# Map loads merged and moved to ScalarE's queue in the final pass of a spectral convolution with hyperbolic normalization

## What is computed

```python
def reference(x, w_re, w_im, bias, gamma, beta):
    x = x + _L0_conv_ref(_gn(x), w_re, w_im, bias)   # group norm, rfft2, 32 x 17 modes mixed per head, irfft2, + bias
    x = x + _L1_conv_ref(_gn(x), gamma, beta)        # group norm, hyperbolic normalization over channels
    return x
```

## Time and profile before

| | us |
|---|---|
| median of 3 runs | 3985.61 (3980.61 to 3986.04) |
| profiled execution, its own time | 4024.94 |
| its span in the trace | 4023.4 |
| busy in the span: PE, DVE, ACT, POOL | 3002.5, 2748.0, 2141.8, 1513.6 |
| TensorE's granted clock, mean | 0.878 of full speed |

### The profile page before, as it was taken

How to read it: one execution, slowest core, us unless ns; L and a number is a source line. 1 busy time by engine, 2 the same in 40 slices (tenths; PEclk the granted TensorE clock), 3 DMA queues, 4 the chain that set the end, 5 groups by cost and what they waited for, 6 DMA issues and landing times. The chain is left out here.

```text
span 4023.4 us, 77883 instructions
## 1 busy us (share of the span) xinstructions
PE 3002.5 (75%) x26018; PEld 1495.1 (37%) x26018; DVE 2748.0 (68%) x2969; ACT 2141.8 (53%) x2940; POOL 1513.6 (38%) x876
## 2 busy tenths in 40 slices
PE   6988898989446767677715877877777778877776
PEld 3555555555211222222203434344333344443332
DVE  1888888888865355555444767677777677777766
ACT  6777676767200011111014767677776677776665
POOL 0110101010111111111113766666666666666666
PEclk9988888988668888888857999999999999999999
DMA  9878777677269999999915989899999899999898
GB/s 373 287 256 282 260 265 274 244 285 253 76 259 354 325 341 376 362 361 374 334 53 183 337 313 329 313 325 321 313 315 320 306 330 334 329 334 311 311 314 288
DMA packets 280512, 1199.08 MB, mean 298 GB/s; under 512 B 35145, under 2 KB 37038, under 8 KB 197934
## 3 DMA queue, kind: packets, MB, share of 16 engines
q1 hardware_dynamic: 266126, 1152.07, 79.9%
q0 software_dynamic: 14112, 43.37, 3.4%
HBM read 883.53 MB, written 311.73 MB: 297 GB/s over the span
## 5 line engine op out<-in xcount | busy, mean ns | idle before, releaser
L1323 POOL TENSOR_TENSOR c_ot<-c_ot,c_pp 128x1024 f32<-128x1024 f32 x512 | 1211.8, 2368 | 727.0 <-DVE c_ot L1272 651.8
L1262 DVE SCALAR_TENSOR_TENSOR c_xt<-c_xt,keep_k,c_p_u 128x1024 f32<-128x1024 f32 x512 | 654.0, 1277 | 332.5 <-DMA c_xt<-in_x 170.8
L1118 PE MATMUL c_p_u<-c_mv,c_zc 64*128 64x256 f32 x4096 | 612.3, 420 | 225.1 <-DVE c_xt L1262 163.1
L1272 DVE SCALAR_TENSOR_TENSOR c_ot<-c_p_f,keep_k,c_xt 128x1024 f32<-128x1024 f32 x512 | 657.3, 1284 | 177.0 <-DMA out<-c_ot 134.4
L1198 ACT ACTIVATE c_pp<-c_p_p,c_cols 128x1024 f32<-128x1024 f32 x512 | 570.5, 1114 | 362.4 <-PE c_p_p L1132 359.0
L1205 ACT ACTIVATE c_sq<-c_xt,c_cols 128x1024 f32<-128x1024 f32 x512 | 584.2, 1141 | 139.5 <-DVE c_xt L1262 138.8
L1118 PEld LDWEIGHTS c_p_u<-c_mv,c_zc 64*128 64x128 f32 x4096 | 371.4, 195 | 532.9 <-DVE c_xt L1262 321.3
L327 ACT ACTIVATE a_junk<-a_xt 128x1024 bf16<-128x1024 f32 x512 | 537.2, 1053 | 28.8 <-DMA a_xt<-in_x 21.5
L246 PE MATMUL a_p_rows<-a_xt,a_dft_h 128*64 128x512 f32 x2048 | 517.5, 652 | 33.6 <-DMA a_bias_t<-in_bias 19.5
L1132 PE MATMUL c_p_f<-c_rt,c_lwc 64*128 64x512 bf16 x1024 | 328.0, 402 | 179.6 <-DVE c_ot L1272 161.3
L663 PE MATMUL b_p_al<-b_xt,b_awc 128*32 128x512 f32 x2048 | 312.4, 682 | 161.2 <-DMA b_xt<-in_x 116.3
(11 more groups left out here) (209 smaller groups left out, 3029.8 us busy)
## 6 DMA issues: line engine op xcount, KB each, us to landing
a_xt<-in_x SPq DMA_DIRECT2D x256, 1024.0 KB, 8.0
b_xt<-in_x SPq DMA_DIRECT2D x128, 2048.0 KB, 16.0
c_xt<-in_x SPq DMA_DIRECT2D x256, 1024.0 KB, 16.7
out<-c_ot SPq DMA_DIRECT2D x256, 1024.0 KB, 18.4
maps<-b_maps POOLq DMA_DIRECT2D x64, 192.0 KB, 5.7
dmap<-b_dmap POOLq DMA_DIRECT2D x16, 768.0 KB, 11.6
c_rt<-maps SPq DMA_DIRECT2D x512, 24.0 KB
c_dmap<-dmap SPq DMA_DIRECT2D x16, 768.0 KB, 17.2
```

The costliest lines, as they stand in the source:

```text
L1118: last = nc.tensor.matmul(p_u[:, 512 * at + W * r:512 * at + W * r + W], zc[t // CH][64 * at:64 * at + 64, i], mv[t % NB][64 * at:64 * at ...
L1262: V.scalar_tensor_tensor(out=u, in0=u, scalar=kc, in1=p_u[:], op0=ALU.mult, op1=ALU.add).then_inc(u_done, 1)
L1272: V.scalar_tensor_tensor(out=ot[t % NB][:, at], in0=p_f[:], scalar=kinv, in1=xt[t % NB][:, at], op0=ALU.add, op1=ALU.mult).then_inc(f_done, 1)
L1323: P.tensor_tensor(o, o, pp[n][:], ALU.add).then_inc(o_done, 1)
```

## The change

The order of the rows in `rt` is changed: a list `MAP_ROWS` gives for each of the three parts a first row and a step, so that the rows of both halves of the partitions lie on one line: 12 rows from 58 in steps of 1, 8 rows from 15 in steps of 14, 4 rows from 36 in steps of 20. The placing of the weights in `misc` follows. The six map loads of a tile become three, each of which fills both halves; the two `bmap` loads stay. All five are issued by ACT, behind `shift(b, t, 1)` and ahead of `square(b, t, 1)`, for tile t + 4 (before: by SP, for tile t + 2), with no wait of their own: `shift(b, t, 1)` has already waited on the `f_mm` that frees the buffer. At the start of the stage ACT waits on `c_in` and issues the loads of four tiles, ahead of its first `copy_part`. SP keeps `x`, the output and the rest, and no longer waits on `c_in` there. The four stores of channel 0 of an image become one.

```diff
+MAP_ROWS = ((58, 1), (15, 14), (36, 20))
...
-    maps_v = io["maps"].rearrange("b m s (t n) -> b t (m s) n", n=TC)
+    maps_v = io["maps"].rearrange("b (a m) s (t n) -> b t a (m s) n", a=2, n=TC)
...
-            def load_maps(b, t):
-                if not (is_at(b, 0) and t < NB):
-                    sp.wait_ge(f_mm, b * GR + 2 * (t - NB) + 2)
...
-                for at in range(2):
-                    for row, rows in ((0, 6), (6, 4), (10, 2)):
-                        sp.dma_start(r[64 * at + row:64 * at + row + rows], maps_v[b, t, 6 * at:6 * at + rows]).then_inc(r_in[t % NB], 16)
-                    sp.dma_start(m[64 * at + M2:64 * at + M2 + 2].rearrange("p (n r) -> p n r", n=2), bmap_v[b, t, at]).then_inc(r_in[t % NB], 16)
...
-                for j in range(4):
-                    sp.dma_start(o0_v[b, 0, j], o0[32 * j:32 * j + 32]).then_inc(o0_out, 16)
+                sp.dma_start(o0_v[b, 0], o0[:]).then_inc(o0_out, 16)
...
-                        load_maps(b, t + 2)
...
-            sp.wait_ge(c_in, 16 * (2 + 2 * NB))
-            for t in range(2):
-                load_maps(0, t)
...
-                    pe.wait_ge(r_in[t % NB], b * (128 * T // NB) + 128 * (t // NB) + 128)
+                    pe.wait_ge(r_in[t % NB], b * (80 * T // NB) + 80 * (t // NB) + 80)
...
+            def load_maps(b, t):
+                if t >= T:
+                    b, t = b + 1, t - T
+                r, m = rt[t % NB], mv[t % NB]
+                for (first, step), rows in zip(MAP_ROWS, (6, 4, 2)):
+                    act.dma_start(r[first:first + step * (2 * rows - 1) + 1:step], maps_v[b, t, :, :rows]).then_inc(r_in[t % NB], 16)
+                for at in range(2):
+                    act.dma_start(m[64 * at + M2:64 * at + M2 + 2].rearrange("p (n r) -> p n r", n=2), bmap_v[b, t, at]).then_inc(r_in[t % NB], 16)
...
                     shift(b, t, 1)
+                    if not (last and t + NB >= T):
+                        load_maps(b, t + NB)
...
             act.wait_ge(zeroed, 2 * NB + 2)
+            act.wait_ge(c_in, 16 * (2 + 2 * NB))
+            for t in range(NB):
+                load_maps(0, t)
             act.wait_ge(filled, 3)
```

More of the change, by code:

```diff
@@ L83, in constants @@
     m[:, 10] = np.where(p // 2 == 0, 1.0, -1.0)
[L84 to L87, removed]
+    for a, at in enumerate((12, 18)):
+        for part, ((first, step), rows) in enumerate(zip(MAP_ROWS, (6, 4, 2))):
+            for i in range(rows):
+                m[first + step * (rows * a + i), at + 2 * part + i % 2] = 1.0
     c["misc"] = m
@@ L1022, in load_x @@
                 sp.dma_start(xt[t % NB][:], x_v[b, t % T] if t < T else x_v[b + 1, t - T]).then_inc(x_in[t % NB], 16)
-            def load_maps(b, t):
-                if not (is_at(b, 0) and t < NB):
-                    sp.wait_ge(f_mm, b * GR + 2 * (t - NB) + 2)
-                if t >= T:
-                    b, t = b + 1, t - T
-                r, m = rt[t % NB], mv[t % NB]
-                for at in range(2):
-                    for row, rows in ((0, 6), (6, 4), (10, 2)):
-                        sp.dma_start(r[64 * at + row:64 * at + row + rows], maps_v[b, t, 6 * at:6 * at + rows]).then_inc(r_in[t % NB], 16)
-                    sp.dma_start(m[64 * at + M2:64 * at + M2 + 2].rearrange("p (n r) -> p n r", n=2), bmap_v[b, t, at]).then_inc(r_in[t % NB], 16)
             def store(b, t):
@@ L1095, in _ @@
             store_channel_0(B - 1)
-            sp.wait_ge(o0_out, B * 64)
+            sp.wait_ge(o0_out, B * 16)
         @block.tensor
@@ L1327, in channel_0 @@
                 if not is_at(b, 0):
-                    pool.wait_ge(o0_out, b * 64)
+                    pool.wait_ge(o0_out, b * 16)
                 P.tensor_tensor(o0[:], th[:], dmap[:, 2], ALU.add).then_inc(o0_ready, 1)
```

## The result

| | before | changed |
|---|---|---|
| median of the runs, us | 3985.82 | 4159.84 |
| ratio to the kernel before | | 1.0405 (1.0316 to 1.0494) |
| the same on another occasion | 3996.92 | 4159.37, ratio 1.0423 (1.0360 to 1.0486) |
| profiled execution, us | 4024.94 | 4136.41 (span 4134.8, clock 0.862) |

What follows compares the result with a forecast made beforehand. Two DMA engines carrying the map rows were taken to bound stage C: 7.26 + 0.33 - 0.25 = 7.34 us a tile, +20 us, plus 6 at the start, giving 4012 us; range 3925 to 4085.

Steps and rivals of the forecast that it cites:

- part 2: Stage C, cost per load: three fewer transfers a tile on the first DMA engines save 0.25 us a tile.
- Which DMA engines set the pace: Stage C: the two engines with the map rows, 160 KB a tile where most carry 128, are the bound.
- Part 1: Stage C, bytes on the first DMA engines: nested loads and the merged store add 7 KB, +0.33 us a tile.
- Part 3: Stage C, ACT with the issue block needs 7.13 us a tile, just under 7.34, leaving it no slack.
- ACT's idle time: Sign of being right: in the body it falls from 30% to under 10%, issues counted.
- part 4: Stage C, SP: losing eight of ten issues is worth nothing, because the DMA engines behind it never run dry.
- Part 5: Start of stage C: ACT issues 20 loads, 8.5 us, before its first copy; +6 us, once.
- Rival C: Stage C: bytes alone count, fewer loads give back nothing, +0.33 us a tile; 4076 us, chance 0.10.
- Rival B: Stage C: ACT becomes the bound at 7.68 us a tile, its queue stopped by backed-up transfers; 4099 us, chance 0.10.
- landing over 14 us: Sign of being right: x in stage C still takes over 14 us from issue to landing.
- 20 closing packets: Sign of being right: closing packets of a group of five loads fall from 28 a tile to 20.
- DMA share near 0.92: Sign of being right: the busy share of the DMA engines stays near 0.92.

Runs made afterwards that it cites:

- e7: Changed kernel with its five merged loads issued by SP and channel 0 in four stores again; 1.0118 of the kernel before.
- f2: e9 with one store of channel 0 in place of four; 0.9984 of the kernel before.
- e9: e6 with ACT's loop over images written out and channel 0 in four stores; 0.9899 of the kernel before.
- n2: Kernel before, but SP loads all twelve map rows three times, to every tenth partition, unused rows weighted zero; 0.9730 of the kernel before, 3878 us.
- n1: Kernel before, but stage B writes all 24 map rows and SP loads them in one plain load; 0.9703 of the kernel before.
- e10: The seven loads of e6 issued by SP instead of ACT, channel 0 in four stores; 0.9889 of the kernel before.
- f1: e5 with channel 0 in four stores; 1.0108 of the kernel before.
- e5: Changed kernel with ACT's loop over images written out, so no back edge and constant addresses; 1.0244 of the kernel before.
- e2: Changed kernel with its five merged loads issued by SP, at the place and with the wait of the kernel before; 1.0116 of the kernel before.
- e3: Changed kernel with the nested 8-row and 4-row loads each split into two plain strided loads, still on ACT; 1.0522 of the kernel before.
- e6: e3 with each of the seven loads going to neighbouring partitions (step 1); 1.0097 of the kernel before.

## Why the prediction was wrong in size and right in sign

4012 us was forecast, 4160 came, outside the range. Two steps of the sum failed: part 2 took off 64 us for fewer loads that the runs do not show, and the back edge of ACT's loop, some 70 us, was in no term.

- **Which DMA engines set the pace: right,** the best part. Where SP issues and channel 0 has four stores a tile takes 6.49, 6.71, 7.09, 7.26 and 7.34 us for 144, 148, 156, 160 and 164 KB. The steps are 0.055, 0.047, 0.043 and 0.02 us per KB; the forecast's price is 0.047. The point at 160 KB is the profile of before, which was 1% above its median.
- **Part 1, +0.33 us a tile for 4 KB of nested loads and 3 KB of store: right for the loads, open for the store.** e7's time is 47 us above the kernel before (0.19 x 256 = 48), though the two traces differ by only 0.08 us a tile (20 us). The store, put at 36 us, measured 34 in f2 against e9, 54 to 57 beside the nested loads on ACT, and nothing beside SP's.
- **Part 2, -0.25 us a tile for fewer loads: wrong.** n2 and e7 have five loads each and give 0.039 us per KB. Beside their line lie n1 with three loads (0.06 us below), e10 with seven (0.07 above) and the kernel before with eight (0.08 above): by the traces, an estimate of 0.03 us a load, a third of what part 2 took. By the runs' times, e7's 47 us are the price of the bytes with nothing given back. This is some 40 to 64 us of the error. What the 1.8 us between 7.26 and 5.5 consist of stays open.
- **Part 3, ACT's floor of 7.13 us: wrong, too high.** I let the block overlap one instruction by 0.4 us; it overlaps two, and f1's tile of 5.42 us holds all five issues. The nested issue was put at 0.55 and took 0.62 to 0.65. ACT's idle time, issues counted, did not fall under 10%: in the changed kernel's body ACT computes 65% of the time and issues 28%, and since these overlap it is idle 20%. So ACT had slack where the forecast saw none.
- **The term that was missing** is the back edge: 5 us for each of 13, about 70 us. I had costed an instruction's duration, not what more instructions do to the loop. That SP's relief is worth nothing (part 4) was not shown by itself; it came with ACT's block, and the two together are nothing. Part 5 was right: 20 issues from 2115.21 to 2125.6, 10 us, and from the first constant load of stage C to DVE's first `add_x` 86 to 92 us pass in the runs with five loads on ACT, against 83 before.
- **The sum again,** by runs that differ in one thing after another, in percent of the kernel before: loads 1.2 (before to e7), issuer -0.1 (e7 to f1), store 1.4 (f1 to e5), back edges 1.6 to 1.8 (e5 to the changed kernel): 4.1 to 4.2, in us 47, -4, 54 and 64 to 72. In another order the store and the back edges come out smaller (34 and 45 us at 156 KB), so these two are prices of this kernel and not of the thing alone.
- **The rivals.** Rival C, bytes alone, 4076 us, is near e5 (4095.67, 1.0244), but that is in part luck: e2 has the same bytes with SP as the issuer and 1.0116. Rival B named ACT as the bound from a block of 2.7 us upward; the block's median is 2.7, but the threshold went down with part 3, and no queue was stopped. With e3's 4.0 us blocks ACT did become the bound.
- **The tests:** landing over 14 us and 20 closing packets came true; the DMA share near 0.92 did not (0.88), and neither did ACT's idle time. These two were the signs that the transfers no longer were the only bound.

## What to carry to other kernels

Count what each DMA engine carries, not the sum: here small loads all began at the first engine, and n2 gained 2.7% by 12 KB less there though it moved 48 KB more in all. Before giving DMA issues to an engine that computes, look at the length of its loop's turn and at its timeline at the back edge; the issues themselves can hide under its arithmetic. A transfer merged with a nested side can fall to two engines; three plain ones of all twelve rows were better here, even though they carry more.

## What the runs showed of the hardware that was not expected

- A loop back edge with a turn of 398 instructions stops ACT for some 6 us (6.47 in the row above, register work included), where it cost 0.2 with 190. SP had one before (3.8 to 6.9 us between the records on either side, 525 a turn) and lost it. It was not wholly hidden: beside SP's stop of 2958.7 to 2965.5 us in the kernel before the DMA engines fell to 31% for 5 us. What it costs is open, since no run has SP's loop written out; that is the next thing to try. Window of the kernel before:

```profile
2965.00:2970.00 5.00, 2.04 (x16) 0.92 (x12) 1.77 (x2) 2.09 (x5) 3.51 (x2) 0.94 0.31 115
```

PE has one as well: its wait for "issue" at `c_p_u`, 13 times each in 2200 to 3850 us, is at most 3.0 us before and 5.3 in n2. Waits view of the kernel before (us in total, times, longest):

```profile
PE c_p_u L1118 <- issue: 33.5, 13, 3.0
```

And of n2:

```profile
PE c_p_u L1119 <- issue: 62.7, 13, 5.3
```

- What an issue costs depends on the step between partitions as much as on nesting: 4 rows took 0.64 us at step 14 (e3) and mostly 0.26 at step 1 (e6), both plain and on ACT; 12 rows took 0.75 us at step 10 (n2) and 0.34 at step 1 (e10), both on SP.
- In f1's and e3's timelines DMA issues begin before instructions that stand ahead of them on the same engine, by up to two of ACT's operations.
